# Another order of the pieces on every engine of a fused eight-layer kernel, and spare products at other places

## The chip, the cores and the metric

The kernel runs on one core of a Trainium2 chip. Its time is the device time of one execution in microseconds (us). Each engine works through its own queue strictly in order: TensorE (PE, with its weight loads as PEld), VectorE (DVE), ScalarE (ACT), GpSimd (POOL) and SyncE (SP), which only issues transfers. They wait for one another through semaphores.

## The reference

One sequence of 2048 rows of 128 numbers goes through eight residual layers. Each layer normalises its input and adds its result to it:

```
x = x + attn_a0(layernorm(x))   # delta rule: state S of 8x8 per head, 16 heads, one step per row
x = x + ffn0(layernorm(x))      # shared + 8 experts, top 2
x = x + attn_b0(layernorm(x))   # top 15 of the causal logits, small MLP on them, palette lookup
x = x + ffn0(layernorm(x))
x = x + attn_a1(layernorm(x))   # linear attention, cumulative sums
x = x + ffn1(layernorm(x))      # 8 experts, top 2, relu squared
x = x + attn_b1(layernorm(x))   # decayed state, one step per row
x = x + ffn1(layernorm(x))
```

The first layer is the one that cannot be cut into independent parts:

```
v_old = einsum('bhd,bhde->bhe', k_t, state)
delta = clip(v_t - v_old, -1, 1)
state = state + clip(0.9 * k_t[..., None] * delta[..., None, :], -1, 1)
o     = clip(einsum('bhij,bhj->bhi', state, q_t), -1, 1)
```

## The kernel before

The rows are 16 tiles of 128. All layers are in flight at once, each some tiles behind the one ahead of it. Every stage is a generator for each engine, cut into pieces by `yield`, and a letter stands for each stage: z prep, f front (q, k, v of the first layer), g gram, s scan, o out, a the first expert layer (called ffn0 in the code), p pal (the logits and the top 15), h near (the gathers), m mix, b the second expert layer, l lin, c and e the third and fourth expert layers (ffn1 in the code), d dec. `fast` (line 501) walks through a string of letters, `ORDER[engine]`, and lets the stage of each letter issue its next piece. So five strings set where each piece stands in each queue; within a stage and an engine the pieces keep their order. The engines meet only at semaphores, which are the same whatever the strings say.

The scan (lines 1005 to 1066 on DVE) does the first layer two rows at a time, 1024 steps: L1033 multiplies, L1041 is a tensor_tensor_scan. Four steps are a block. For each block there is a round trip to PE: L1013 (DVE) transposes the last results, L610 (PE) multiplies them with the keys, L1049 (DVE) masks the product, L621 (PE) multiplies that with the keys two blocks on, and L1056 (DVE) adds the result to the values of that later block. L1049 stands after the second step of a block, L1056 after the fourth, so PE has a few steps' time for each. On PE the pieces s with L610 and L621 stand between the pieces of all other stages.

Other lines that are spoken of: L764 (Gram matrices of the gathered rows), L797 and L810 (last products of mix), L831 and L834 (cumulative sums of lin), L564 (transposes of normalised tiles), L871 and L880/L881 (products of the ffn1 experts), L929 and L892 (last products of dec and ffn1), all on PE; L1873 (the gathers, 15 for each tile), L1885 and L1891 (mix), L1733 and L1738 (normalisation), L1898, L1905 and L1914 (lin), L1933 and L1939 (dec) on POOL; L1196 (second search of the top 15), L1220 (clip of mix) and L1249 (adds mix to the tile) on DVE. On SP, L2030 loads the cosines of a tile, L2036 stores its rows of the gather table, L2042 stores its distances, L2053 loads them again for mix, and L2061 stores a finished tile.

`FILL` holds one digit for each of the 2250 pieces on PE. Before each piece `fill(n)` (line 550) sets `idle[0]` to its digit; the next call of `bank` (line 533), which takes one of four PSUM banks in turn, first issues that many spare products (line 541, ones times ones, 128x512, bf16, the result is never read) into the bank and then sets `idle[0]` to 0. The spare products stand after the wait for the bank and ahead of most waits for operands. A piece that takes no bank issues none, and the next piece overwrites its digit.

Of the kernel before, what the change touches and what calls it, by code (L numbers as in the profile page):

```python
# [92 lines left out]
def pieces(stage):  # L93

    for k, _ in enumerate(stage):
# [20 lines left out]
        "smgpmmaplmslmaapmsgmcccmcssccmsmcscsmcmfssmeseeeammsmeseedassedsaesddfdgaaamsddsmmmdpmdbsmbommsbsmpmsmmpsooo"
        "obmbbsmbsbfsbmmslspolossppgslmlllmsallamasmmmsmlmslgmmmsmfcccasmmmscasmaccsccssacafsaeseeespmeemsmdesbedempd"
        "msdssmmbbdpmgsopdmsmmmdddbbobsobsbbooslgfslsmsssllollsloslmsmmpmslglspamspasmcascmsmmccgpmmccsmmcsmcscmasaem"
        "eemsadmemseedfesddadasaesfemdsmdsmmmbmmpmsddgbbsmsmommpsfpbsoosbobsobbsbmmsgsmmsspmlsolmsmosppsmslllmlallsma"
        "fmmgagslmmsmlmfmmcspmsamcccccssaascasaasccgmsmmmseeesemmdmseemmmsmesmdsbdsdbdsebeofspdpdddoobsopbobsgbbbmmss"  # L120
        "lmsmlmsmmsmmsmmmslpslollospppllagamsamspmmlmlfsmgmmcsfcsacascccscsccasasaaseeeesmemedsesedmsesmmdsmdbbmsmdsp"
        "bpggddosmddmmmbosobsbobomsbsbmmsmssmmsplmlosmmmsmposllspmsalslllapsaflssplmmmccmcccgmsmmcmgcscscaaaseeedesmm"
        "meemmmsasaeamsedseddsbdbpbsmpdsdsmmmddmbosbfgboosomosbsbbsfsmmmlslpsmmommsmosppsmllllsallsmsgaaspmfsllmsmggm"
        "mcscccsmmmcpcmascascascaasaeseeseesemmsmdeesdsedsdmmmspmmbdbbpsmdfomdmmddsbbbososbboobfmsgslslsmsmomoslslsml"
        "plsllspmspmlflpsgmcacsmmcmmspcccmmcgsccmsamsaesemesmmmeegdesesedsadsedgsdasammmmmmmdfmdsdadsaasmmsmosmbbbsoo"
        "oospbsbbfpbsmsbbsmmosmsmlsmlsmmmspommsfgmslslslllplmsgmlsmlmspacsmacccscmmsmscascsscspcpgsgemmeemmemmemdmddd"
        "mmseemmmeadsaaseaasgaodsdsddbssbmbssoosoombspbpbsmbbsmmmsmbmpsmmmopolpslsmssmslallalllsmmalmslsmmmcsppcccccs"
        "ccceeeedsmmmmseemmmeaemdsaseadddsaasmammmddbsddsbbommmpmoobpbobobbbmmmmmlpmmmlmspmplllllolopplmalmaammcccccm"
        "mccccaaeedadeddemedemmmmaaeeadsemmmddbdbbpmmmmmpmbmbmbpbbbpmmmpbplmbblmmmmpmmllllbllbmbmbbblmmlmmllcccccclll"
        "llcclcleleedededdemdmemmemmemmmmmcmmmcdmdddcbmbbcmmmmmcmmcmbbcbmbbbcmcmlmdlmmmmededdedelllllleemmmmmmmmedded"  # L130
        "ldelmmmmcccccbbbccccbbebeeedbebbededlldedllllllelldddcdccccccccedeededdedeeeddeddeeeeeeeee",
    "DVE":
# [62 lines left out]
        "lopooloollllllachhmhmhhedhmhhhdhddhdbphhhhpppppbllllllllhhhlhchhlllhlmlmlledhhmhhhdhdchddhbldelmlmllddmdllld"  # L195
# [4 lines left out]
FILL = (  # L200
    "091909062040000000025030020020010000010010000100100000010000500001020020000070000901000001020000000000000020"
# [1974 lines left out]
```

How the kernel before makes its waits and increments, by code:

```python
    def wait_ge(self, sem, val):  # L69
        if self.seen.get(id(sem), 0) < val:
            self.seen[id(sem)] = val
            self.engine.wait_ge(sem, val)
# [460 lines left out]
        def bank(key, *until):  # L533
            b, old = bk.take(key, *until)
            held.extend(old)
            if idle[0]:
                free()
                w.wait_ge(*PV.at("b1", 0))
            for _ in range(idle[0]):
                e.matmul(b[:, 0:512], onesb[:, :], onesb[:, :].unsqueeze(1).to_broadcast([128, 4, 128]), start=True, stop=True)
            idle[0] = 0
            return b
# [1 line left out]
        def free():  # L545
            for sem, val in held:
                w.wait_ge(sem, val)
            held.clear()
# [4 lines left out]
        def norm(s, c):  # L553
            yield
            b = bank((s.name, "T", c), s.A.at("xt", c))
            if s.raw:
                w.wait_ge(*s.src(c))
            elif s.scaled:
                w.wait_ge(*s.A.at("xn", c))
            else:
                w.wait_ge(*s.G.at("xn", c))
            w.wait_ge(*loaded("ident"))
            free()
            e.transpose(b[:, 0:128], X[:, s.tile(c), :] if s.raw else s.xn[c % 2][:, :], ident).then_inc(*s.P("T"))
# [1 line left out]
        def front(c):  # L566
            yield from norm(f, c)
            yield
            b = bank(("front", "qkv", c), f.A.at("pv", c))
            w.wait_ge(*loaded("bias"))
            w.wait_ge(*loaded("cst"))
            free()
            e.matmul(b[:, 0:384], ones, bias[:, 0:384], start=True, stop=False)
```

## Time and profile before

| | us |
|---|---|
| median of 3 runs | 1384.04 (1383.59 to 1386.72) |
| profiled execution | 1393.87 |
| its span in the trace | 1392.1 |
| PE busy | 1243.0 |
| DVE busy | 1000.2 |
| POOL busy | 910.7 |
| ACT busy | 820.1 |

The span is the time from the first instruction to the last; the rest of the profiled execution, 1.8 us, lies around it. A PE record's end is modelled, so a busy PE is not one that works at its peak. The last scan step of the kernel starts 1140.4 us into the span; up to there all stages share the engines, and behind it the last tiles run out.

### The profile page before, as it was taken

The numbers are of one execution on the slowest core, as the hardware profiler recorded it, in microseconds if no ns is written. First come the engines' busy times: TensorE is split into PE (matmuls) and PEld (weight loads), VectorE is DVE, ScalarE is ACT, GpSimd is POOL, SyncE is SP. The second block draws the span as 40 slices with busy tenths as digits, with TensorE's granted clock in tenths as the row PEclk, the third lists the DMA queues.
The fourth block names the chain that finished last, engine by engine and source line by source line (L and its number), as shares of the span: only waits on it lengthen the run. The fifth ranks groups of instructions, "written<-read, shape, count | busy, mean of one in ns | idle before, by whom it ended". The sixth has DMA issues, their size and how long they took to land. (4 is left out here: it accounts for less than half of the span.)

```text
span 1392.1 us, 47171 instructions
## 1 busy us (share of the span) xinstructions
PE 1243.0 (89%) x18561; PEld 813.5 (58%) x18561; DVE 1000.2 (72%) x4437; ACT 820.1 (59%) x2193; POOL 910.7 (65%) x1321
## 2 busy tenths in 40 slices
PE   7777797989999998998899999999999999998896
PEld 3333454656566575756656665755666565757654
DVE  3768878778777868787786888978888775464432
ACT  2232253556676576757476666657574657667764
POOL 5353668686968677685776676776857466674541
PEclk8687678989999999999999999999999999999998
DMA  6000101001000000000010000100001010101000
GB/s 175 2 1 5 30 12 31 24 15 28 12 20 19 16 21 11 24 15 19 14 27 12 15 24 8 29 8 23 15 6 32 6 39 10 34 15 31 4 3 7
DMA packets 27257, 29.35 MB, mean 21 GB/s; under 512 B 12146, under 2 KB 22291, under 8 KB 27027
## 3 DMA queue, kind: packets, MB, share of 16 engines
q0 software_dynamic: 8336, 16.73, 4.9%
q1 hardware_dynamic: 18690, 9.51, 2.5%
q8 instruction: 149, 2.44, 0.8%
q14 instruction: 82, 0.66, 0.2%
HBM read 24.90 MB, written 2.29 MB: 20 GB/s over the span
## 5 line engine op out<-in xcount | busy, mean ns | idle before, releaser
L1873 POOL DMA_INDIRECT sb<-table,sb x240 | 241.8, 1007 | 81.5 <-issue 51.1
L1041 DVE TENSOR_TENSOR_SCAN ps<-ps,sb 128x47 f32<-128x47 f32 (+3 forms) x1024 | 271.0, 265 | 30.5 <-ACT sb L1445 1.5
L1033 DVE TENSOR_TENSOR ps<-sb,ps 128x24 f32<-128x24 f32 (+3 forms) x1024 | 193.1, 189 | 14.7
L541 PE MATMUL ps<-sb 128*128 128x512 bf16 x585 | 177.6, 413 | 8.7 <-ACT sb L1658 2.7
L1733 POOL TENSOR_TENSOR sb<-sb 128x1 f32<-128x1 f32 x128 | 73.2, 574 | 138.3 <-DVE sb L976 137.6
L610 PEld LDWEIGHTS ps<-sb 32*32 32x32 f32 x2032 | 41.0, 108 | 107.6 <-DVE sb L1013 65.6
L610 PE MATMUL ps<-sb 32*32 32x32 f32 x2032 | 69.8, 209 | 36.2 <-DVE sb L1013 35.6
L621 PEld LDWEIGHTS ps<-sb 32*32 32x32 f32 x2032 | 41.5, 108 | 93.1 <-DVE sb L1049 54.3
L982 DVE TENSOR_TENSOR sb<-ps,sb 128x128 f32<-128x128 f32 x112 | 32.2, 289 | 80.5 <-PE ps L708 29.8
L541 PEld LDWEIGHTS ps<-sb 128*128 128x128 bf16 x585 | 54.7, 105 | 58.8 <-issue 14.5
L1369 ACT ACTIVATE sb<-ps 128x128 f32<-128x128 f32 x128 | 34.9, 275 | 90.7 <-PE ps L564 90.2
L621 PE MATMUL ps<-sb 32*32 32x12 f32 x2032 | 64.7, 189 | 19.0 <-DVE sb L1049 10.0
L1056 DVE TENSOR_TENSOR ps<-sb,ps 128x12 f32<-128x12 f32 x254 | 40.9, 161 | 51.7 <-PE ps L621 50.3
L708 PE MATMUL ps<-sb 128*128 128x128 f32 x512 | 77.3, 298 | 0.0
L1670 ACT ACTIVATE sb<-ps,sb 128x128 bf16<-128x128 f32 x256 | 70.8, 375 | 8.2 <-PE ps L881 8.0
L596 PE MATMUL ps<-sb 128*128 128x480 f32 x128 | 73.8, 665 | 1.4 <-DVE ps L1056 0.5
L1049 DVE TENSOR_TENSOR sb<-ps,sb 128x32 f32<-128x32 f32 x254 | 45.9, 181 | 39.2 <-PE ps L610 38.1
L1885 POOL TENSOR_TENSOR sb<-sb 128x512 f32<-128x512 f32 (+1 forms) x32 | 47.3, 1485 | 36.0 <-DVE sb L1239 35.8
L764 PE MATMUL ps<-sb 128*16 128x16 f32 x4096 | 64.6, 211 | 6.3 <-issue 4.2
L708 PEld LDWEIGHTS ps<-sb 128*128 128x128 f32 x512 | 68.9, 209 | 1.9 <-issue 1.1
L1772 POOL TENSOR_TENSOR sb<-sb 128x480 f32<-128x480 f32 x64 | 66.0, 1034 | 4.9 <-ACT sb L1408 4.3
L764 PEld LDWEIGHTS ps<-sb 128*16 128x16 f32 x4096 | 54.3, 133 | 24.8 <-issue 18.4
(313 smaller groups left out, 3532.3 us busy)
## 6 DMA issues: line engine op xcount, KB each, us to landing
sb<-table,sb POOLq DMA_INDIRECT x240
sb<-in_cs SPq DMA_DIRECT2D x16, 128.0 KB
table<-sb SPq DMA_DIRECT2D x17, 64.0 KB, 1.5
sb<-dscr SPq DMA_DIRECT2D x64, 2.0 KB
out<-sb SPq DMA_DIRECT2D x16, 64.0 KB, 1.6
sb<-in_x SPq DMA_DIRECT2D x3, 256.0 KB, 5.4
sb<-in_wex SPq DMA_DIRECT2D x1, 512.0 KB, 4.1
sb<-in_rvx SPq DMA_DIRECT2D x1, 512.0 KB, 4.5
```

Of the source, the lines that this page charges most:

```text
L541: e.matmul(b[:, 0:512], onesb[:, :], onesb[:, :].unsqueeze(1).to_broadcast([128, 4, 128]), start=True, stop=True)
L596: e.matmul(b[:, 0:32 * LW], blk, g_.pp[j % 2][:, :], start=True, stop=True).then_inc(*g_.P("s"))
L610: x = e.matmul(psS[rows, 0:32], KZT[c % 2][rows, 32 * o1:32 * o1 + 32], R[g % 2][rows, :], start=g == 0, stop=True, skip_group_check=True)
L621: x = e.matmul(b[rows, 0:12], SB[g % 2][rows, :], KM[c2 % 2][rows, 4 * o2:4 * o2 + 4, :].rearrange("p a b -> p (a b)"), start=True, stop=True)
L708: x = e.matmul(b[:, 0:128], s.hw[j // 4][:, 128 * (j % 4):128 * (j % 4) + 128], wex[:, 128 * j:128 * j + 128], start=False, stop=j == 7)
L764: x = e.matmul(pb[32 * q:32 * q + 16, 16 * k:16 * k + 16], PTt[:, at, :], PTt[:, at, :], start=True, stop=True)
L1033: e.tensor_tensor(at(psP, p + ROW - 3 - 2 * m, [ROW, 3], [2, m], [1, 2]), AC[:, row(n, k), :, HIST - 2 * m:HIST].rearrange("p r (a b) -> p ...
L1041: e.tensor_tensor_scan(at(psD, 16 + k + COMB * skip, [COMB, 3 * ROW - skip]), at(psP, p + skip, [1, 3 * ROW - skip]), Q[:, i % 32, skip:3 ...
L1670: x = e.activation(s.w[:, 128 * at:128 * at + 128], bk.of[s.name, "d", g, c][:, 128 * j:128 * j + 128], ACT.Copy, scale=t[:, 40 + at:41 + at])
L1733: e.tensor_tensor(st[:, 11:12], st[:, 10:11], mhalf[:, 0:1], ALU.pow).then_inc(*s.G("lr"))
L1772: e.tensor_tensor(g_.pp[j % 2][:, :].rearrange("p (a b c) -> p a b c", b=2, c=LW), at(KT[c % 3], 32 * j, [2, 16], [0, 2], [1, LW]), km[:, ...
L1873: e.indirect_dma_start(GA[:, k, :], None, table[0:128 * i + 128, :] if i else table0, bass.IndirectOffsetOnAxis(u[:, k:k + 1], 0)).then_in ...
```

## The change

Both tables are replaced, `ORDER` and `FILL`; no other line changes. Each string of `ORDER` holds the same letters in the same numbers (2250 on PE, 3861 on DVE, 1707 on ACT, 996 on POOL, 80 on SP). 897 pieces of PE, 1419 of DVE, 866 of ACT, 585 of POOL and 55 of SP stand at another place, most of them one or two places on.

```diff
 ORDER = {
...
     "POOL":
...
-        "cbedllllldllldddceddddde",
+        "cbedllllllllddddceddddde",
     "SP":
-        "ppppmpppmpppmppmpppmppppmppppmppmppppmpmpppppmpmpppmppepemeppppmpeepemeeeeeeeeee",
+        "pppppmpmpppppmpmppppmpppmeppmppeppmpppmpppmpppepmepmpeppmppepmpppeppmepmeeeeeeee",
 }
 FILL = (
...
```

The digits of `FILL` add up to 585 before and to 1242 now. All 585 stand at pieces that take a bank. Of the 1242, 587 do; the other 655 stand at pieces that take none, and are overwritten.

On PE, some 850 us into the span, in the part where all stages run. L610 and L621 are the scan's two products, L764 and L831/L834 belong to mix and lin. Before:

```order
L736 MATMUL ps<-sb 128x512 x2
L610 MATMUL ps<-sb 32x32 x4
L764 MATMUL ps<-sb 16x16 x16
L831 MATMUL ps<-sb 128x432
L834 MATMUL ps<-sb 128x432
L831 MATMUL ps<-sb 128x360
L834 MATMUL ps<-sb 128x360
L621 MATMUL ps<-sb 32x12 x4
```

And now:

```order
L736 MATMUL ps<-sb 128x512 x2
L610 MATMUL ps<-sb 32x32 x4
L831 MATMUL ps<-sb 128x432
L834 MATMUL ps<-sb 128x432
L621 MATMUL ps<-sb 32x12 x4
L764 MATMUL ps<-sb 16x16 x16
L564 MATMUL ps<-sb 128x128
L831 MATMUL ps<-sb 128x360
```

The 16 products of L764 and one pair of L831 and L834 (360 columns) moved from ahead of the scan's L621 to behind it.

On PE, some 655 us into the span; L871 and L564 belong to the last ffn1 and to dec, L797 and L810 to mix. Before:

```order
L871 MATMUL ps<-sb 128x128 x4
L797 MATMUL ps<-sb 32x16 x16
L564 MATMUL ps<-sb 128x128
L797 MATMUL ps<-sb 32x16 x8
L610 MATMUL ps<-sb 32x32 x4
L871 MATMUL ps<-sb 128x128 x8
L797 MATMUL ps<-sb 32x16 x8
L541 MATMUL ps<-sb 128x512 x3
L810 MATMUL ps<-sb 32x128 x16
L621 MATMUL ps<-sb 32x12 x4
```

And now:

```order
L797 MATMUL ps<-sb 32x16 x8
L871 MATMUL ps<-sb 128x128 x4
L810 MATMUL ps<-sb 32x128 x8
L871 MATMUL ps<-sb 128x128 x4
L610 MATMUL ps<-sb 32x32 x4
L810 MATMUL ps<-sb 32x128 x8
L621 MATMUL ps<-sb 32x12 x4
```

The scan's L610 moved behind the last eight of L797, behind both groups of L871 and behind the first eight of L810, and three spare products are gone from this place.

On POOL, 1263 to 1272 us into the span, the last gathers of the last tile (L1873). Before:

```order
L1933 COPY sb<-sb 128x4
L1873 DMA sb<-table,sb 128x128
L1939 TENSOR_TENSOR sb<-sb 128x4x128
L1733 TENSOR_TENSOR sb<-sb 128x1
L1738 TENSOR_SCALAR sb<-sb 128x128
L1873 DMA sb<-table,sb 128x128
L1933 COPY sb<-sb 128x4
L1939 TENSOR_TENSOR sb<-sb 128x4x128
L1873 DMA sb<-table,sb 128x128
```

And now:

```order
L1933 COPY sb<-sb 128x4
L1939 TENSOR_TENSOR sb<-sb 128x4x128
L1873 DMA sb<-table,sb 128x128 x2
L1733 TENSOR_TENSOR sb<-sb 128x1
L1738 TENSOR_SCALAR sb<-sb 128x128
L1933 COPY sb<-sb 128x4
L1873 DMA sb<-table,sb 128x128
L1939 TENSOR_TENSOR sb<-sb 128x4x128
```

The last gather stands ahead of the second L1939 instead of behind it.

## Rows read from the trace of the kernel before

**Rows 1.** The page: busy time of PE and DVE, and the spare products' group.
```profile
PE 1243.0 (89%) x18561; PEld 813.5 (58%) x18561; DVE 1000.2 (72%) x4437; ACT 820.1 (59%) x2193; POOL 910.7 (65%) x1321
...
L541 PE MATMUL ps<-sb 128*128 128x512 bf16 x585 | 177.6, 413 | 8.7 <-ACT sb L1658 2.7
```

**Rows 2.** Four stretches: PE, PEld, DVE, ACT, POOL busy, clock, DMA share, GB/s.
```profile
0.00:315.00 315.00, 253.85 (x3249) 141.28 (x3253) 230.53 (x1194) 121.80 (x341) 191.95 (x326) 0.79 0.13 33
315.00:1141.00 826.00, 766.83 (x12286) 517.86 (x12287) 655.65 (x2926) 533.20 (x1416) 588.68 (x837) 0.97 0.07 19
1141.00:1314.00 173.00, 159.61 (x2564) 113.02 (x2563) 88.90 (x236) 119.20 (x306) 109.44 (x133) 1.00 0.08 20
1314.00:1392.00 78.00, 62.71 (x471) 41.34 (x471) 25.12 (x84) 45.87 (x132) 20.67 (x27) 0.95 0.02 5
```

**Rows 3.** Scan steps (L1041) in two early stretches: busy time (count), clock.
```profile
35.00:70.00 35.00, 12.75 (x48) 0.67 0.01 2
70.00:105.00 35.00, 9.60 (x36) 0.84 0.01 1
```

**Rows 4.** Timeline of PE late in the span: five spare products in a row.
```profile
1357.73 1.24 PE L541 MATMUL ps<-sb 128*128 128x512 bf16 x5
```

**Rows 5.** Waits of DVE for the scan's products, whole span: us, times, longest.
```profile
DVE ps L1056 <- PE ps L621: 50.3, 65, 3.1
...
DVE sb L1049 <- PE ps L610: 38.1, 52, 4.8
```

**Rows 6.** Timelines at 850 us: PE, then DVE; in brackets idle before, releaser.
```profile
850.58 0.77 PE L831 MATMUL ps<-sb 128*128 128x360 f32 x2
...
851.88 0.25 PE L621 MATMUL ps<-sb 32*32 32x12 f32 x8
...
852.20 0.18 DVE L1056 TENSOR_TENSOR ps<-sb,ps 128x12 f32<-128x12 f32 x1 [1.90 <-PE ps L621]
```

**Rows 7.** Timelines at 655 us: PE, then DVE.
```profile
655.44 0.26 PE L610 MATMUL ps<-sb 32*32 32x32 f32 x8
...
657.34 1.10 PE L810 MATMUL ps<-sb 32*32 32x128 f32 x32
...
656.17 0.17 DVE L1049 TENSOR_TENSOR sb<-ps,sb 128x32 f32<-128x32 f32 x1
...
659.05 0.18 DVE L1056 TENSOR_TENSOR ps<-sb,ps 128x12 f32<-128x12 f32 x1 [1.70 <-PE ps L621]
```

**Rows 8.** The chain that ended last, at the last gather: start, us, what.
```profile
1269.45 1.18 POOL sb L1939
...
1270.78 2.64 DMA sb<-table,sb
1273.46 0.66 PE ps L751 x4
```

**Rows 9.** The same chain where mix of the last tile ends.
```profile
1309.00 0.71 PE ps L929 x4
...
1311.43 1.95 PE ps L810 x64
```

**Rows 10.** Timeline of POOL at 1340 us.
```profile
1339.42 1.13 POOL L1933 COPY sb<-sb 128x4 f32<-128x4 f32 x1
...
1344.56 0.18 POOL L1933 COPY sb<-sb 128x4 f32<-128x4 f32 x1
```

**Rows 11.** SP's issues at 143 and 184 us, and the clip that waits.
```profile
143.15 2.46 SPq L2053 DMA_DIRECT2D sb<-dscr  x4
184.69 0.34 SPq L2036 DMA_DIRECT2D table<-sb  x1
...
190.22 0.74 DVE L1220 SCALAR_TENSOR_TENSOR sb<-ps,sb 128x512 f32<-128x512 f32 x1
```

**Rows 12.** The last tile: its second search (timeline of DVE), a later gather (chain).
```profile
1239.29 2.29 DVE L1196 FIND_INDEX8 sb<-sb 128x8 uint32<-128x2048 f32 x1
...
1255.88 0.94 POOL sb L1873
```

More of the change, by code:

```diff
@@ L116 @@
[L116 to L120, printed above, removed]
@@ new lines @@
+    "ACT":
+        "ffffffffffgfgfsffsffzzgfffgzffgfzsfzsfgzfffggszfffsfzfgooozooffoozffgoffaazasaaagassgpppfppffffpsopgopofoopo"
+        "posgoaaaaasaafpffmfgmpsfpmmopgfpppffffpoooosoommfmsgomamfmppafpfaaapaffmmasgpmgpsooooosofffffommmmppoppgpsaa"
+        "apfagaapmmsgpmmamfpmfbffbbmmbbbbpsfpmlollgooooloslfffffomlmmmgplpppoppccfcccccppacccccsagccamadmfaaspmmdddda"
+        "dfmffgmmfmbsbgbbobbffffgofpbompoosoolllgmomfmlpplmpalgppplaaasgacpccccsacccmccccmpccmmfeepeeeeaeedeemeedemed"
+        "dmddmfffsgbbfobmbbppbooobomosoffmmfffmfplpolplppplagallalasaampgpmmcpmfccaccccscmcmcccccmmffefeseeeeeeedbeed"
+        "eebeddddfbbbpmgpbobooosooolgfflffflmllolmmppmsaplgpapapfcccaacccccgamcccmpccmcsmaeedeeeeedemsemddeefededmmeb"
+        "ffffbpmgbbpobbpffspffbfoooooommgmmplppposlflppalallafgaagamlmmmpfcfafccsccmcmcccccccpmmcfpgeedeeeemeeesedbee"
+        "eddbddbebbfofbffpfsbooopogoommlmmllpppolplpfppsalamagaammmlafgcmcfcffmsccacccccccpccmmeeeedeeeeebeseedeeddfb"
+        "ddbppbbpbggmoboooooosmmmmspplppllolpaapllpafffaaalffmcmmcpcmcccccgccccmcgcmmameeedeeeesdeeeeeeesddpdbfdbpbbb"
+        "mpbbofgoooooomfffmlsmmpsplpolpppafllalagaapfalffffmmmspggmccccccccccamcmcccmmeeedeeeeeeepeebsdeeddddpmbfbbbs"
+        "pofbboooooofffmlgllmmompplflpslpapplfpffffgcccccccaccmccsmccpcgammeadeeeaaeeefdeegeemeeepddsmaddmgmmfobbbbbb"
+        "oooopboofffpsfmmmmsollpplpfpfgfffllplmagmlmfmcpacaccccccsccmmaccaccmppmageegeeeeeddeeddseedmeedmapeobgbbmbbb"
+        "soooomobppompppoplpplalsmmallalmmalaamcpsccpcccccccccmccmmeeedeedeeeeeeeeaeddddmpbbbbbommbpmmobopoopopolpllm"
+        "mpppllolppalmaamcacaccccacmccccmcccmamedeedddeeddeeeeeeeeembbpbbpbpbmbmmpmpppbppblpbbblblpmmlbllmmllmmllcccc"
+        "ccccclcclccclmmleedeedeeeddeededeeeemcpcmmcmcbbcmbbbccbcccbccmccmlmmddllmmdeededdeememleleeeleemeelcccbccccb"
+        "ccbcbbcbcccbeeedeeeeeedeeddelellddellllccccccccccccccdeedeeeeddeddeeeeeeeeeeeeeeeeeeeee",
@@ L219 @@
[L219 to L221 removed]
+    "903199061040000000025030024120103000010010000000100103010020500001120020030070000900000130020000103200000020"
+    "200002000200000003000000000000401000000002100500002100034000000002300610000030004320010000000030040020000000"
@@ new lines @@
+    "101003000020000010000311013011301200013030003301100000000020030103102000000000100401200520000000000000000210"
+    "000000000000320003023300011400000000030000000000001300000003000600000110000300201000000000000002030033030000"
+    "000400000030000000202200100000000000004010072600020000030100000000000000000000000000030000000000000000000000"
+    "000000000000000000003000000220100120000000001000374050000600020000200000004000000100101000009000000000600060"
+    "300000000000000020000020000000000700000040001100000000200000000000000000003022000000003010303003120330020000"
@@ new lines @@
+    "000000000007000000000014000000005000030000020002200023000101004002000000000010000000000000000100100000000100"
+    "000001000003000000000000000000000000000000000000006210001633000000000000000000000000000000000000000002000000"
+    "000000200000000000000010000000500000002101000101012000000010000007502000100000000000013800030000000000000000"
+    "400000000007130000000003000000000000200004000200000000000100001000000020000510000040006030030000103002200020"
+    "000000001000000000000000000000020000000000000000400000003000000000000702020002010000060026303030800106000020"
```

173 lines of the change are left out of this document (75 added, 98 removed).

## The prediction

> **What bounds the kernel now.** I read the page's busy times first: PE is busy for 1243.0 of 1392.1 us and DVE for 1000.2 [rows 1]. A busy share over the whole span hides where the time goes, so next I cut the span at the end of the scan and at two points beside it [rows 2]. From 315 to 1141 us, where all stages run, PE is busy for 766.8 of 826 us (93%) and DVE for 655.7 (79%). In this part PE comes nearest to a bound, and the scan on DVE is the chain that it must not hold up. Up to 315 us PE is busy for 253.9 (81%) and DVE for 230.5 (73%). Behind 1141 us there is no scan; the chain of waits runs back through POOL, PE and single transfers there [rows 8, 9], and from 1314 us every engine but PE is less than 60% busy: that is one tile's latency.
>
> The view of waits then tells what DVE waits for: in the whole span 50.3 us for L621 (65 times) and 38.1 us for L610 (52 times), the two products of the scan's round trip [rows 5]. These 88.4 us are the largest sum that an order on PE can give back to the scan, and any product put ahead of L610 or L621 can add to it.
>
> **The spare products.** The change speaks of 1242 in place of 585. A digit of the table counts only where its piece takes a bank; counted in the two built orders, L541 stands 585 times before and 587 times now. Five of them in a row take 1.24 us [rows 4], 0.25 us each, so the two more cost 0.5 us of PE at most, and where PE waits anyway they cost nothing; I take 0. If all 1242 were issued, 655 x 0.25 = 164 us of products would go into a PE that idles for 149 us in all; that case is shut out by the order. Most digits that did change place moved with a neighbour, because two pieces changed places and the product stands with the first bank taken.
>
> The clock belongs here, since the products keep PE at work. The granted clock is 0.79 up to 315 us and 0.97 from there to 1141 us [rows 2]. With the levels 1.2 and 2.4 GHz that is 2 x 0.21 x 315 = 132 us and 2 x 0.03 x 826 = 50 us at the lower one. What does it cost? From 35 to 70 us the clock is 0.67 and 48 scan steps are done; from 70 to 105 us it is 0.84 and only 36 are done [rows 3]. So early on the clock does not set the pace, and I price it at 0 there. In the middle, with PE at 93%, the 50 us can cost up to half of themselves, 25 us. The Trainium skill, "TensorE: Matmul & The Clock Gate", section "HAM oscillation — how this bites in real kernels", puts the cost of throttled time at half of it wherever it falls. By that rule the early 132 us would cost 66 us and each early spare product would be worth having; rows 3 speak against it for this kernel.
>
> **The moves on PE.** For each scan product that DVE waited for I set the work that the new order takes from ahead of it, or puts there, at its duration in the trace, with what that work waits for held at its old time. Three results come of it, of which one sample each can be followed.
> - Products that come earlier. At 850 us, L621 loses 16 of L764 and a pair L831/L834 from ahead of it. The pair alone takes from 850.58 to 851.88, 1.3 us; with L764 it is 1.7 us of the 1.90 us for which DVE waited [rows 6]. Capped at its wait each time, this sums to 13.6 us over the span.
> - Waits that grow: 5.7 us, none above 1.4 us.
> - New waits where there was none: 11.3 us over 21 places. The largest in this sum, 3.3 us, is at 655 us: L610 went behind two groups of L871 and eight of L810. L810 could not start before 657.34, and L1049 took the product at 656.17 [rows 7]. Read on, though: the eight of L810 (half of 1.10 us) and four of L871 end at about 658.2, so L1049 comes at 658.5, 2.3 us late; the 1.70 us for which L1056 waited after it vanish in this, and L1056 comes at 659.7 in place of 659.05. Of 3.3 us, 0.65 are left.
>
> So a gain stays, while a loss is partly swallowed by the next wait. I take the gains in full and the losses (17.0 us) at a third, between the fifth of the sample and all: 13.6 - 5.7 = 7.9 us. Of these I let half reach the end, since the scan shares its pace with PE, which saves no work: -4.0 us. The ends are -13.6 (all gains, no loss) and +17.0 (the reverse).
>
> **The moves on POOL behind the scan.** The last gather of the last tile is issued at 1270.78, right behind L1939 (1.18 us); it lands 2.64 us later and PE takes it at 1273.46 [rows 8]. The new order puts L1939 behind the gather: 1.2 us earlier. Late next is the previous tile: L929 waits for POOL's products of dec until 1309.00, and L810 of the last tile, 1311.43, stands behind L929 [rows 9]. The new order leaves this sequence on PE. So between 0 and 1.2 us come through; I take 0.6. At 1339.42 a copy of four columns, L1933, takes 1.13 us, six times the 0.18 us of its like at 1344.56 [rows 10]. Three L1914 stood behind it; it now stands behind them. That is worth 0 to 1.1 us; I take 0.5 us, since L1939 of the dec layer comes later by as much and ends against the same normalisation. Sum -1.1 us.
>
> **Moves priced at nothing, with their cover.** SP stores finished tiles from 480 us on instead of from 1082 us; each add that it waits for is done before the next transfer of SP is due, so nothing queues behind it. The first L2053 moves from 143.15 behind the L2036 of 184.69: four issues of 2.46 us end at 187.5, and L1220 reads at 190.22 [rows 11]. That leaves 2.7 us for the landing; if it takes longer, L1220 and the scan step behind it wait, up to 2 us. On DVE, the first part of an expert pick, which ran behind the second search (L1196, 1239.29 to 1241.58) before, now stands ahead of it. I allow it until the time at which it ran, so the search ends some 4.5 us later, at 1246; the first gather that needs it is issued at 1255.88 [rows 12], and POOL is busy with other pieces until then. All other moves on ACT, POOL and DVE take 0; bounded by the nearest rows, the PE sums above, -13.6 to +17.0 us.
>
> **Sum.** 1393.87 - 4.0 - 1.1 = 1388.8 us in terms of the profiled execution. That one ran 0.7% above the median of the runs, 1384.04; in their terms the sum is 1388.8 x 1384.04 / 1393.87 = 1379.0 us.
>
> **The rivals.**
> 1. Nothing that can be measured: gains and losses on the scan cancel. For it: the sums are 13.6 and 17.0 us, and the work is the same on each engine. Against it: the swallowed loss at 655 us. Time 1384.
> 2. Slower: the scan's products stand behind work that waits for another engine. The place is PE from 640 to 1090 us; besides 655 us, an L610 near 784 us now follows L845, L773, L779 and L564, which wait for ACT and for an add. With all losses counted (17.0) and all gains (13.6) it is +3.4 us, with half the gains (6.8) it is +10.2; the middle, +6.8, gives 1400.7, in the runs' terms 1391. It decides once a late product isn't followed by a wait that was there already, as the one at 659.05 was [rows 7]. Against it: 16 of the 21 new waits are under 0.6 us.
> 3. The clock. If the spare products at their new places hold the clock for 20 of the 50 us at 1.2 GHz between 315 and 1141 us, half of that comes back: 1383.9, or 1374. The same can go the other way (from 1066 to 1150 us there are 12 fewer of them): +7 us, 1391.
>
> **How the numbers follow.** No change means within 0.2% (2.8 us), about what a measurement of this kernel can tell. The forecast has 0.34, its own range is 1372 to 1381; the clock as a gain has 0.10: faster 0.44. Rival 1 has 0.27. Rival 2 has 0.22 and the clock as a loss 0.07: slower 0.29. The range goes from 1368 (gains of 13.6 in full and a little of the clock) to 1394 (rival 2 with half the gains): about one in ten is left out on each side.
>
> **What would show it.** The waits of DVE for L621 and L610 should sum to 80 us or less in place of 88.4; the wait of 1.90 us at 850 us should be gone, and near 655 us L1049 should wait for L610 by about 2 us with no wait at L1056 behind it. The last scan step should start some 4 us ahead of 1140.4. L541 should stand 587 times. Of the last two L1939 ahead of the last gather one should be left behind it. I am wrong if these waits sum to 90 us or more (rival 2), if the clock from 315 to 1141 us leaves 0.97 by more than 0.01 (rival 3), or if the last scan step comes early and the end doesn't: then the tail after 1141 us gave it back.

## The result and the profile after

The changed kernel takes 1397.81 us (median of 17 runs, 1392.61 to 1407.67), the kernel before 1389.32 us beside it (17 runs, 1383.17 to 1398.24). The ratio is 1.0069, with a 95% interval of 1.0051 to 1.0088: slower by 0.7%, where I had forecast 1379 us and faster (a ratio of 0.996 to the 1384.04 us of before that I started from). The time lies 4 us beyond the end of the range. Of the 18.8 us between forecast and measurement 5.3 are not the change's: the kernel before itself took 1389.32 us in these 17 runs and 1384.04 in the three ahead of the prediction.

The two profiled executions are no measure of this difference. That of before took 1393.87 us, 4.5 us above its median, and that of the changed kernel 1393.32 us, 4.5 us below its own. So I read from the traces where time moved, and from the timed runs how much.

First the page of the changed kernel, which answers to [rows 1]:

```profile
PE 1235.9 (89%) x18563; PEld 818.3 (59%) x18563; DVE 998.7 (72%) x4437; ACT 821.2 (59%) x2193; POOL 904.9 (65%) x1321
```

L541 stands 587 times in the changed kernel's list of groups, as counted. DVE is busy for 998.7 us in all, a little less than the 1000.2 of before: whatever slows the kernel isn't a larger sum of work on DVE. Next the four stretches, which answer to [rows 2]:

```profile
0.00:315.00 315.00, 253.13 (x3380) 142.39 (x3384) 235.38 (x1221) 125.34 (x355) 194.95 (x336) 0.82 0.13 33
315.00:1141.00 826.00, 761.58 (x12162) 519.54 (x12152) 648.09 (x2887) 531.19 (x1400) 577.90 (x824) 0.96 0.07 18
1141.00:1314.00 173.00, 159.46 (x2572) 114.65 (x2571) 90.09 (x249) 119.00 (x308) 111.27 (x136) 1.00 0.07 19
1314.00:1392.00 78.00, 61.76 (x469) 41.76 (x468) 25.19 (x83) 45.69 (x132) 20.75 (x27) 0.95 0.02 5
```

Up to 315 us DVE has done more than before (1221 instructions for 1194), from 315 to 1141 us less (2887 for 2926). At 1.2 GHz (twice the missing share of the granted clock, times the length) the trace of before has 198 us in all, this one 195. From 315 to 1141 us alone it is 57 us before and 72 now (0.97 and 0.96), 15 more. Some 12 of these lie behind scan step 609, where this trace is no slower (the table below), and 3 in the stretch where the time is lost. So the loss is in the middle, and it is hardly the clock. The view of DVE's waits answers to [rows 5]:

```profile
DVE ps L1056 <- PE ps L621: 46.1, 59, 3.5
DVE sb L1049 <- PE ps L610: 41.3, 60, 3.3
```

They sum to 87.4 us, where before had 88.4 and I had named 80 or less. Both sampled places moved the way that I had worked out, but less far. Of the wait of 1.90 us near 850 us [rows 6], which should have gone, 0.67 is left, and near 655 us [rows 7] L1049 now waits, 1.07 us in place of about 2, and L1056 no longer does (groups of one instruction: start, duration, in brackets the idle time before it and its releaser):

```profile
854.02 0.17 DVE L1056 TENSOR_TENSOR ps<-sb,ps 128x12 f32<-128x12 f32 x1 [0.67 <-PE ps L621]
```

```profile
661.33 0.19 DVE L1049 TENSOR_TENSOR sb<-ps,sb 128x32 f32<-128x32 f32 x1 [1.07 <-PE ps L610]
...
662.93 0.17 DVE L1056 TENSOR_TENSOR ps<-sb,ps 128x12 f32<-128x12 f32 x1
```

**Where the scan falls behind.** The scan has 1024 steps (L1041), in one order in both kernels, so the start of step n can be set against the start of step n. Worked out from these starts, for the kernel before, the changed one and some of the experiments below (us for each part):

```
steps        before  changed  changed, again (e5)  e9     e10    e11    e12
0 to 357     306.6   300.6    305.5                304.7  302.0  301.0  301.1
357 to 383   28.3    30.0     28.4                 30.0   28.3   29.8   29.5
383 to 391   10.6    13.2     13.6                 13.2   10.6   13.2   11.0
391 to 577   220.5   223.9    223.8                226.6  222.8  222.9  220.3
577 to 586   10.9    13.3     14.9                 13.8   10.9   13.7   10.9
586 to 609   21.5    22.5     22.5                 21.9   22.3   21.7   22.9
609 to 1023  517.0   514.3    514.4                512.2  513.8  514.8  510.6
```

e9 has the new order from about step 357 to 609 alone and e10 the old order there alone; e11 has the new order around the two short places of steps 383 to 391 and 577 to 586 alone, e12 the old order around these alone. So in the first row e9 and e11 are in the old order, as before is: the same order took between 301.0 and 306.6 us, and the 6 us that the changed kernel is ahead at step 357 in its trace can't be put down to the change. With the 2.7 us of the last row and 3.0 behind the scan they hide its loss in this one trace, whose whole span is no longer than that of before (1391.5 for 1392.1 us).

Steps 357 to 609 (331.6 to 623.4 us in the trace of before) take 291.8 us before and 302.8 after. Here are this window and two short ones, of the two places, of before, then of the changed kernel, with the busy time of the scan steps alone in them (252, 8 and 9 steps) and the clock:

```profile
331.60:623.40 291.80, 66.45 (x252) 0.97 0.07 18
359.90:370.50 10.60, 2.12 (x8) 1.00 0.03 8
591.00:601.90 10.90, 2.38 (x9) 1.00 0.08 20
```

```profile
325.70:628.50 302.80, 66.56 (x252) 0.97 0.07 18
355.70:368.90 13.20, 2.08 (x8) 0.92 0.06 16
592.70:606.10 13.40, 2.38 (x9) 1.00 0.11 28
```

The same steps, the same busy time, 11 us more around them at the same clock. Two short places make 5.0 of it. There DVE is busy for longer and idle for less: 12.4 and 0.7 us for 8.9 and 1.7 at the first, 12.4 and 0.9 for 9.7 and 1.2 at the second. Outside them it is idle for longer; over the whole of steps 357 to 609 the waits for L621 and L610 sum to 21.8 us for 18.7. What DVE does at the second, first in the changed kernel and then in the kernel before:

```profile
593.32 0.27 DVE L1041 TENSOR_TENSOR_SCAN ps<-ps,sb 128x51 f32<-128x51 f32 x1
593.50 0.15 DVE L1144 MAX8 sb<-sb 128x8 f32<-128x8 f32 x1
593.56 1.78 DVE L1147 SCALAR_TENSOR_TENSOR sb<-sb 128x256 f32<-128x256 f32 x1
595.27 0.28 DVE L1249 TENSOR_TENSOR sb<-ps,sb 128x128 f32<-128x128 f32 x1
595.47 3.03 DVE L1152 SCALAR_TENSOR_TENSOR sb<-sb 128x256 f32<-128x256 f32 x1
598.42 0.19 DVE L1033 TENSOR_TENSOR ps<-sb,ps 128x42 f32<-128x42 f32 x1
```

```profile
592.13 0.42 DVE L1147 SCALAR_TENSOR_TENSOR sb<-sb 128x256 f32<-128x256 f32 x1 [0.61 <-ACT sb L1493]
...
592.84 0.88 DVE L1152 SCALAR_TENSOR_TENSOR sb<-sb 128x256 f32<-128x256 f32 x1
```

DVE is "busy" here and no wait is shown, but one instruction of one shape takes 0.42 us in one trace and 1.78 in the other, and the next 0.88 and 3.03. (The trace of before isn't free of this at the place: L1130 takes 1.11 us in it, at 595.17, and 0.17 in the changed kernel.) POOL in the changed kernel at this time:

```profile
593.45 1.03 POOL L1772 TENSOR_TENSOR sb<-sb 128x480 f32<-128x480 f32 x1
594.43 0.63 POOL L1760 TENSOR_TENSOR sb<-sb 128x256 f32<-128x256 f32 x1
595.02 0.76 POOL L1780 TENSOR_TENSOR sb<-sb 128x224 f32<-128x224 f32 x1
595.75 0.42 POOL L1784 TENSOR_TENSOR sb<-sb 128x16 f32<-128x16 f32 x2
596.13 2.08 POOL L1795 TENSOR_TENSOR sb<-sb 128x512 f32<-128x512 f32 x2
598.37 0.98 POOL L1873 DMA_INDIRECT sb<-table,sb  x1 [0.16 <-issue]
```

Seven instructions without a gap, from 593.45 to 598.21 us. L1152 starts at 595.47 and ends at 598.50, 0.29 us behind the last. Here is POOL in the kernel before. L1152 started at 592.84 there, beside L1780, and ended at 593.72, ahead of both L1795; L1760 took 0.86 us for the 0.63 above:

```profile
592.39 0.59 POOL L1780 TENSOR_TENSOR sb<-sb 128x224 f32<-128x224 f32 x1
592.95 0.42 POOL L1784 TENSOR_TENSOR sb<-sb 128x16 f32<-128x16 f32 x2
593.34 0.86 POOL L1760 TENSOR_TENSOR sb<-sb 128x256 f32<-128x256 f32 x1
594.16 2.09 POOL L1795 TENSOR_TENSOR sb<-sb 128x512 f32<-128x512 f32 x2
```

The Trainium skill, "SBUF — State Buffer", section "Who interferes with whom", has the rule: a DVE instruction with two inputs in SBUF contends with a GpSimd (POOL) instruction that reads SBUF, and one of the two is blocked whole. The traces agree as to which instructions: at the two places L1147, L1152, L1130 and L1132 are the stretched ones, all sb<-sb, while L1249 and the scan's own, with an operand in PSUM (ps), keep their times. The first place is alike. In the changed kernel POOL runs there from 359.53 to 365.18 us without a gap; L1152 takes 1.33 us at 359.57 (0.38 before), and L1130 and L1132, 128x8 each, take:

```profile
362.03 1.28 DVE L1130 TENSOR_TENSOR sb<-sb 128x8 f32<-128x8 f32 x1
363.35 1.86 DVE L1132 TENSOR_TENSOR sb<-sb 128x8 f32<-128x8 f32 x1
```

where the trace of before has 0.17 us for each. The scan's steps stand behind them in DVE's queue. The four stretched lines together take 3.7 us more than before at the first place and 2.6 us more at the second, and the places last 2.6 and 2.4 us longer.

### The profile page after: what moved, and what is told of

It reads as the page before. It is cut to its first block, busy times and chain, and to the rows that moved or that the text cites. A ratio compares the mean times of both kernels' runs of the same rounds, so it can differ in the third digit from the quotient of the medians.

```text
span 1391.5 us, 47171 instructions
## 1 busy us (share of the span) xinstructions
PE 1235.9 (89%) x18563; PEld 818.3 (59%) x18563; DVE 998.7 (72%) x4437; ACT 821.2 (59%) x2193; POOL 904.9 (65%) x1321
## 4 chain that ended last, share of the span: by engine, by line
PE 47%; POOL 19%; DVE 13%; issue 11%; ACT 8%; SPq 1%; DMA 1%; POOLq 0%; DVEq 0%; ACTq 0%
POOL sb L1873 5%; PE ps L541 4%; PE ps L708 3%; PE ps L764 3%; DVE ps L1041 3%; PE ps L596 2%; DVE ps L1033 2%; PE ps L621 2%; POOL sb L1733 2%; PE ps L831 2%; PE ps L610 2%; PE ps L736 2%; PE ps L640 2%; PE ps L788 2%; POOL sb L1885 1%
## 5 line engine op out<-in xcount | busy, mean ns | idle before, releaser
L1041 DVE TENSOR_TENSOR_SCAN ps<-ps,sb 128x47 f32<-128x47 f32 (+3 forms) x1024 | 271.7, 265 | 30.1 <-ACT sb L1445 1.1
L1873 POOL DMA_INDIRECT sb<-table,sb x240 | 242.6, 1011 | 75.8 <-issue 52.3
L541 PE MATMUL ps<-sb 128*128 128x512 bf16 x587 | 177.0, 412 | 6.9 <-ACT sb L1572 1.4
L610 PE MATMUL ps<-sb 32*32 32x32 f32 x2032 | 69.5, 208 | 38.0 <-DVE sb L1013 36.2
L610 PEld LDWEIGHTS ps<-sb 32*32 32x32 f32 x2032 | 40.5, 107 | 104.3 <-DVE sb L1013 61.8
L621 PEld LDWEIGHTS ps<-sb 32*32 32x32 f32 x2032 | 41.5, 108 | 97.9 <-DVE sb L1049 56.0
L621 PE MATMUL ps<-sb 32*32 32x12 f32 x2032 | 64.9, 188 | 26.4 <-DVE sb L1049 15.1
L541 PEld LDWEIGHTS ps<-sb 128*128 128x128 bf16 x587 | 54.0, 104 | 56.1 <-issue 14.9
L1049 DVE TENSOR_TENSOR sb<-ps,sb 128x32 f32<-128x32 f32 x254 | 46.0, 181 | 42.7 <-PE ps L610 41.3
L1056 DVE TENSOR_TENSOR ps<-sb,ps 128x12 f32<-128x12 f32 x254 | 40.8, 161 | 47.3 <-PE ps L621 46.1
L764 PE MATMUL ps<-sb 128*16 128x16 f32 x4096 | 63.5, 211 | 5.2 <-issue 3.9
L764 PEld LDWEIGHTS ps<-sb 128*16 128x16 f32 x4096 | 53.8, 133 | 23.7 <-issue 17.2
```

The costliest lines, as they stand in the source:

```text
L541: e.matmul(b[:, 0:512], onesb[:, :], onesb[:, :].unsqueeze(1).to_broadcast([128, 4, 128]), start=True, stop=True)
L610: x = e.matmul(psS[rows, 0:32], KZT[c % 2][rows, 32 * o1:32 * o1 + 32], R[g % 2][rows, :], start=g == 0, stop=True, skip_group_check=True)
L621: x = e.matmul(b[rows, 0:12], SB[g % 2][rows, :], KM[c2 % 2][rows, 4 * o2:4 * o2 + 4, :].rearrange("p a b -> p (a b)"), start=True, stop=True)
L764: x = e.matmul(pb[32 * q:32 * q + 16, 16 * k:16 * k + 16], PTt[:, at, :], PTt[:, at, :], start=True, stop=True)
L1041: e.tensor_tensor_scan(at(psD, 16 + k + COMB * skip, [COMB, 3 * ROW - skip]), at(psP, p + skip, [1, 3 * ROW - skip]), Q[:, i % 32, skip:3 ...
L1873: e.indirect_dma_start(GA[:, k, :], None, table[0:128 * i + 128, :] if i else table0, bass.IndirectOffsetOnAxis(u[:, k:k + 1], 0)).then_in ...
```

## The experiments

Three theories at first: M, the scan's products on PE wait in the middle, C, the spare products and the clock, and T, the tail behind the scan. Then, for the spare products apart from the order: O, the order makes the loss by itself, B, the new places of the spare products are worse, and J, spare products cost when moved away from the order that they stand in. Last W and P (the loss sits between 331 and 623 us, in the two places above) against J. Hybrids were cut by the trace: a piece is in the new order if it ran in the window, and its digit goes with it. "Chip A" below stands for the chips on which the kernel before takes 1390 us, as where the change was timed, "chip B" for those on which it takes 1454 to 1460 us. Each ratio is to the kernel before in the same group, on the same chip, with its 95% interval.

**e1 to e4, parts of the change on the kernel before (chip B).** The edit of e1 starts so in PE's string; e2 and e3 are alike further on, and e4 changes only the table of digits:

```diff
 "PE":
-"sfffsggffssgzzgssfssgsfsssszsgsssfzsssszssgssszssgsfsszsgoszoosossssfzfgssozossosasasasgsssaassasasasasgsssp"
+"fssffggffssgzzgssfssgsfsssszsgsssfzsssszssgssszssgssfszsgoszoosossssfzfgsoszossosasasasgsssaasassasasasgsssp"
...
 FILL = (
-"091909062040000000025030020020010000010010000100100000010000500001020020000070000901000001020000000000000020"
+"903199061040000000025030024120103000010010000000100103010020500001120020030070000900000130020000103200000020"
...
```

> The kernel before, with the new order of PE, DVE, ACT and POOL and its spare products only for the pieces that ran up to 315 us; every later piece, and SP, stands as before. The loss of the whole change is 0.69%, some 9 us. Theory M (the loss comes from the scan's products between 315 and 1066 us, where the changed kernel fell 8 to 10 us behind in the two traces): this one is 0 to 4 us faster, ratio 0.997 to 1.000, since the changed kernel was 4 us ahead at 315 us. Theory C (the clock: other places of the spare products cost something wherever they move): slower by its share, some 2 us, ratio 1.001 to 1.003. Theory T (the tail): 1.000.

> The kernel before, with the new order and the spare products that go with it only for the pieces that ran from 315 to 1066 us. Theory M (the scan's products wait there): nearly the whole loss is in here, 7 to 11 us, ratio 1.005 to 1.008. Theory C (clock): two thirds of it, ratio 1.003 to 1.005. Theory T (tail): 1.000.

> The kernel before, with the new order and its spare products only for the pieces that ran from 1066 us on. The prediction took 1.1 us off for the two moves on POOL here. Theory M: ratio 0.998 to 1.000. Theory T (the tail carries the loss; it has 18 spare products less than before): ratio 1.004 or more. Theory C: 1.001 to 1.003.

> The order of before on every engine; only the table of spare products is the new one, each digit on the piece on which the changed kernel has it (587 are issued, some 1 in 3 of them at another piece). Theory M and the prediction: no effect, 0.999 to 1.001. Theory C (the spare products and the clock): it carries the loss, ratio 1.004 or more; if it carries part of it, the ratio is that part.

Measured: e1 1476.07 us, ratio 1.0096 (1.0063 to 1.0128); e2 1507.20, 1.0319 (1.0294 to 1.0344); e3 1473.30, 1.0084 (1.0061 to 1.0107); e4 1474.22, 1.0084 (1.0055 to 1.0112). No theory had all of this (C named e4's, T e3's): each part costs, and the middle more than three times as much as the whole change on chip A. The baseline, 1460.48 us, says that something else is at work. It is seen in PE's waits; here those of e4, whose order is that of before (waiter, releaser: us in total, times, longest):

```profile
PE ps L797 <- issue: 9.3, 17, 1.2
PE ps L610 <- issue: 4.8, 6, 1.2
PE ps L788 <- issue: 4.8, 9, 1.2
PE ps L764 <- issue: 4.7, 6, 1.5
```

"Issue" is idle time in which the engine waited for nothing that the profile shows. The trace of before on chip A has 4.2 us of it at L764, 1.6 at L788 and none at L797. So these four say little of the loss on chip A.

**e5 to e8, the order and the spare products apart (chip A).** e5 is the changed kernel once more; e6 has its order with the digits of before on their pieces; e7 and e8 have none:

```diff
 FILL = (
-"091909062040000000025030020020010000010010000100100000010000500001020020000070000901000001020000000000000020"
+"000000000000000000000000000000000000000000000000000000000000000000000000000000000000000000000000000000000000"
...
```

> The changed kernel itself, unaltered, beside the other kernels of this group, since the kernel before took 1460 us on the chip of the first group and 1389 us on the one where the change was timed. All theories: ratio about 1.007 if the loss is the same on this chip; on the chip of the first group, where parts of the change cost 0.8 to 3.2%, it may be up to 1.02.

> The order of the changed kernel on every engine, with the spare products of before, each on the piece on which it stood before (585 issued). Theory B (the new places of the spare products are simply worse): this one is back at 1.000 to 1.003. Theory J (the spare products are fitted to the order that they stand in, and cost when moved away from it): it is slower than the changed kernel, 1.010 or more. Theory O (the order makes the loss and the spare products don't matter): it is the same as the changed kernel.

> The kernel before with none of its 585 spare products. Left out is work whose results nothing reads. By the prediction the products cost nothing and the clock is worth up to 25 us in the middle: 1.00 to 1.03. If time at 1.2 GHz costs a third of itself, as the scatter over the runs of the first group says (0.12 to 0.48 us of span for each us at the lower clock), and such time grows from 200 to some 500 us: ratio 1.05 to 1.10.

> The changed kernel with none of its 587 spare products. With e7 it compares the two orders alone. Theory O (the order): it is 0.5 to 1% slower than e7. Theories B and J (the spare products and the clock): the two are equal within 0.3%, or this one is faster, as the waits that the prediction summed would have it (-4 us, -0.3%).

Measured: e5 1402.87 us, 1.0094 (1.0057 to 1.0131); e6 1407.04, 1.0115 (1.0075 to 1.0155); e7 1450.32, 1.0427 (1.0393 to 1.0460); e8 1450.23, 1.0427 (1.0396 to 1.0459). e6 takes theory B away: the old digits don't help the new order. Its ratio is what J asked for (1.010 or more) and, within the noise, also that of the changed kernel, as O had it. e7 and e8 are equal, each to about 0.35%. That is what J had said, and not O, which had e8 slower by 0.5 to 1%: without spare products a loss of the order of up to some 0.5% could hide there, but hardly all of 0.94%. In single traces e8 is still 0.8 and 2.5 us slower than e7 at the two places above (15.9 for 15.1, 15.9 for 13.4), with L1152 at 3.03 us for 0.87 at the second; why the whole kernels are equal all the same is open. e7 came out between its two stated ranges (up to 1.03, and from 1.05). They also price the clock. e7 in the four stretches:

```profile
0.00:315.00 315.00, 227.18 (x3168) 135.30 (x3168) 232.14 (x1199) 123.10 (x346) 193.57 (x328) 0.74 0.13 33
315.00:1141.00 826.00, 732.80 (x11519) 514.98 (x11509) 618.86 (x2810) 512.88 (x1351) 560.38 (x805) 0.88 0.07 17
```

Over its runs e7 has 483 us at 1.2 GHz, before 195 beside it (twice the missing share of the granted clock times the span, mean of the runs). The span grows by 60 us for these 288: 0.21 us for each, with the gain from 585 products less already taken off. Early, DVE does as much in 315 us at 0.74 (1199) as before did at 0.79 (1194), so the price of 0 there stands; from 315 to 1141 us it does 116 instructions fewer.

**e9 to e12, windows of the order (chip A).** e9 is the kernel before with the new order at 331 to 623 us, e10 the changed kernel with the old order there; e11 and e12 are the same pair for the two places alone. At the second place e11 moves on POOL:

```diff
-L1772 TENSOR_TENSOR sb<-sb 128x480
-L1873 DMA sb<-table,sb 128x128
-L1780 TENSOR_TENSOR sb<-sb 128x16x14
-L1784 TENSOR_TENSOR sb<-sb 128x16 x2
-L1760 TENSOR_TENSOR sb<-sb 128x256
+L1873 DMA sb<-table,sb 128x128
+L1772 TENSOR_TENSOR sb<-sb 128x480
+L1760 TENSOR_TENSOR sb<-sb 128x256
+L1780 TENSOR_TENSOR sb<-sb 128x16x14
+L1784 TENSOR_TENSOR sb<-sb 128x16 x2
 L1795 TENSOR_TENSOR sb<-sb 128x512 x2
```

The gather (L1873), which had stood inside the row of tensor instructions, now stands ahead of it, and seven of them follow one another. On DVE L1144 goes behind three more scan steps and L1147 behind one more, and both come to stand beside this row.

> The kernel before, with the new order of PE, DVE, ACT and POOL and its spare products only for the pieces that ran from 331 to 623 us (scan steps 357 to 609), which took 291.8 us before and 302.8 to 304.8 us in three traces of the new order. Theory W (the loss is made in this part and stays): 8 to 12 us slower than before, ratio 1.006 to 1.009. Theory J (the loss is that of any order that the spare products were not fitted to, wherever it is): the ratio says nothing of this part, and this kernel and e10 are both slower than before, by 1.005 or more.

> The mirror of e9: the changed kernel, with the order and the spare products of before only for the pieces that ran from 325 to 628 us. Theory W: it loses nothing, ratio 0.997 to 1.002. Theory J: as slow as the changed kernel or slower, 1.007 or more.

> The kernel before, with the new order only for the pieces that ran at 355 to 371 us and at 586 to 606 us, where two-input instructions of DVE on SBUF wait behind unbroken chains of POOL in the new order (L1152 takes 3.03 us at 595 us and 0.88 before; L1130 and L1132 take 1.28 and 1.86 us at 362 us and 0.17 each before). Theory P (these places): the stretched L1152 is seen again, the two places together cost 5 to 8 us, ratio 1.003 to 1.006. Theory J: stretched instructions may be there, but the time is anywhere. No effect of them on the end: 1.000 to 1.002.

> The mirror of e11: the changed kernel with the order of before only for the pieces at 350 to 369 us and at 586 to 608 us. Theory P: it wins back 5 to 8 us of the changed kernel's loss, ratio 1.001 to 1.004, and L1152 near 595 us is under 1 us. Otherwise it stays at 1.007 to 1.009.

Measured: e9 1399.91 us, 1.0074 (1.0059 to 1.0089); e10 1393.20, 1.0026 (1.0009 to 1.0044); e11 1392.23, 1.0025 (1.0010 to 1.0040); e12 1391.80, 1.0013 (0.9993 to 1.0033). Theory W has e9 where it expected it and e10 just outside; J, which wanted both at 1.005 or more, has only e9. The changed kernel (1.0069, 1.0094) with 763 of some 8800 places in the four strings put back is within 0.2 to 0.3% of before. And e12, with 76 places put back, wins back at least as much as e10 with ten times as many, within the noise of the two. (The changed kernel wasn't timed beside them; its 1.0069 and 1.0094 come from two other groups with the same time of before, 1389 to 1390 us.) e11 brings in 3.5 us of what e12 takes away: the lower end of its range missed by a little, so in the old order the places cost about half. On this chip the longest L1152 follows the order at the place. All L1152 from 320 to 640 us (shortest, median, longest in ns), in e11 and in e12:

```profile
L1152 DVE SCALAR_TENSOR_TENSOR sb<-sb x9: 414/424/3032, 329.7 to 629.0; 128x256 f32<-128x256 f32 x9
```

```profile
L1152 DVE SCALAR_TENSOR_TENSOR sb<-sb x9: 381/424/877, 330.0 to 622.9; 128x256 f32<-128x256 f32 x9
```

The median is one and the same; only the longest moves, 3.03 us with the new order at the place and 0.88 with the old. The waits of e12 on DVE, beside [rows 5]:

```profile
DVE ps L1056 <- PE ps L621: 40.5, 57, 3.0
DVE sb L1049 <- PE ps L610: 38.3, 55, 3.3
```

They sum to 78.8 us, below the 80 that I had named (e10: 81.8; changed and e5: 87.4 and 88.2). So in the new order part of these waits goes with the two places. That doesn't hold the other way: e11, which has the places in the old order, sums to 85.6, less than the 88.4 of before. Nor is it shown that the places cost time behind them as well: steps 391 to 577 take 223.9 us in the changed kernel and 220.3 in e12, but 222.8 in e10, with the old order there and at the first place.

DVE's busy time on the page says the same of the places in both orders. It is 1003.4 us in e11 for 1000.2 before, and 994.5 in e12 for 998.7 and 1000.2 in the two traces of the changed order. It also shows what the ratios leave unexplained:

```profile
PE 1232.0 (89%) x18557; PEld 815.4 (59%) x18557; DVE 994.5 (72%) x4437; ACT 820.8 (59%) x2193; POOL 902.3 (65%) x1321
```

e12 has 5.7 us less on DVE than before, and 9.6 us less in the waits for the scan's products, and still is no faster (1.0013). Something else in the new order gives this back. It wasn't found.

**e13 to e18, which engines at the two places, and a better kernel (chip B).** e13 and e17 are one kernel, e12 with only DVE and POOL put back; e14 puts back only PE and ACT; e15 is e12 with the old order from 1143 us on; e16 and e18 are e15 with the old order also from 369 to 451 and 861 to 891 us. Of e13 the edit on DVE at the first place:

```diff
-"sssssssssdsssddsssdsmsfsmaassssssssssssssmssssabssdssssssssfsssssssssssssbsssssssssssbpbsbbssfbsssbfssssbsss"
+"sssssssssdsssddsssdsmsfsmaassssssssssssssmsssabssssdsssssssfsssssssssssssssssssssssbsbpbbbsfsssfbsbsssssbsss"
```

> e12 with less in it: the changed kernel with the order of before only on DVE and POOL, only for the pieces at 350 to 369 us and 586 to 608 us; PE, its spare products and ACT stay new. Theory P (the loss at the two places is DVE's two-input SBUF instructions standing behind POOL's chains): the whole gain of e12 is here, ratio 1.000 to 1.003, and the sum of L1130, L1132 and L1152 from scan step 357 to 609 is back to 10 us from 13. Theory Q (it is PE's order at these places): ratio stays at 1.006 to 1.009.

> The other half of e12: order of before only on PE (with its spare products there) and ACT at the two places; DVE and POOL stay new. Theory P: ratio 1.005 to 1.009, L1152 near 595 us takes 3.03 us again. Theory Q: 1.000 to 1.003.

> e12 and also the order and the spare products of before for all pieces from 1143 us on, behind the scan. In single traces the stretch from the last scan step to the end took 251.6, 251.5 and 250.0 us with the old order there and 248.6, 252.4, 252.0 and 253.1 with the new. If the prediction's -1.1 us for this stretch is right, this one is 1 us slower than e12 (ratio 1.002); if the traces are, it is 1 us faster (1.000), which is less than five rounds can tell, so the trace decides.

> A version meant to beat both: e15, with the order of before also from 369 to 451 us and from 861 to 891 us, where the new order lost 2.0 and 2.1 us in the trace of e12 against before. If such local losses and gains add up: scan steps end 12 us ahead of before (e12: 8.8), ratio 0.993 to 0.998. If an order is only good as a whole with its spare products: 1.002 or more.

> The kernel of e13 once more: its group ran on a chip on which the kernel before took 1454 us and every kernel in the new order 3.6 to 4.5% more, so it could not be set against e12, which ran where before takes 1390 us. On such a chip, theory P (DVE behind POOL's chains): ratio 1.000 to 1.003. Theory Q (PE's order at the two places): 1.006 to 1.009. From the traces of e13 and e14, where each half took back a part (scan steps 383 to 391 took 11.56 and 12.02 us; 13.2 with all new, 10.6 with all old), a third: half of the gain, 1.003 to 1.006.

> The kernel of e16 once more, for the same reason. If local losses and gains add up: the last scan step is 10 to 14 us ahead of that of before, ratio 0.993 to 0.998. If an order is only good as a whole with its spare products: 1.002 or more.

Measured: e13 1521.22 us, 1.0437 (1.0394 to 1.0481), and e17 1518.72, 1.0444 (1.0413 to 1.0474); e14 1522.89, 1.0447 (1.0399 to 1.0494); e15 1510.01, 1.0389 (1.0346 to 1.0433); e16 1505.04, 1.0356 (1.0309 to 1.0403), and e18 1498.89, 1.0313 (1.0279 to 1.0347). Both groups fell on chip B, where all kernels in the new order lose 3 to 4.5%, so no range for a gain was met (e16 and e18 lie in their other range, 1.002 or more, which on chip B says nothing). What is left is their order and their traces. Steps 383 to 391 and 577 to 586 take 12.1 and 13.9 us on chip B with the new order on all engines (e2), 12.0 and 13.4 in e14, 11.6 and 12.5 in e13, and 10.6 and 10.9 in e15 with all four engines put back. Each half takes back a part, DVE and POOL more of it, and neither the whole. L1152 at the second place tells why an order on DVE and POOL alone doesn't settle it. In e13 both are in the old order, and from 320 to 720 us the longest is 2.73 us (2.72 in e17):

```profile
L1152 DVE SCALAR_TENSOR_TENSOR sb<-sb x9: 380/424/2730, 364.2 to 687.6; 128x256 f32<-128x256 f32 x9
```

It starts at 652.85 us there, beside L1760 on POOL (652.62), and ends at 655.58, behind both L1795; in the trace of before it had started beside L1780 and ended ahead of them. By these traces what decides is when the two engines meet, and not their own two orders alone. That DVE and POOL alone would win the change back on chip A was not measured. No kernel here beat the kernel before.

## Why the prediction was wrong

- **The step that failed** is in the moves priced at nothing: "All other moves on ACT, POOL and DVE take 0". I bounded them by sums on PE and asked of each moved instruction only what waits for it. I didn't ask what else runs while it runs. Putting the old order back at two places, 76 of the changed places, gives 0.6 to 0.8% back (e12 at 1.0013 against 1.0069 and 1.0094), about the whole loss; the new order at these places alone costs 0.25% (e11). At once they cost 2.6 and 2.4 us. On DVE, steps 357 to 609 hold 5.5 us more of busy time (236.3 for 230.8) and 5.5 us more of idle time. The trace of before already showed such a stretch (L1152 0.88 us at 592.84, with another of its kind at 0.38). The Trainium skill, "SBUF — State Buffer", section "Who interferes with whom", has the rule. That the order at these places costs the time is shown. That it does so by the stretched instructions is read from the traces, where they account for the 5.0 us at once; that these 5.0 become the 8 to 11 us of e12 is not explained. The places hold moves on all four engines, and putting back two of the four took back only a part (e13, e14). Nor is it the sum of the stretches over the kernel: DVE is busy for 1.5 us less than before in all.
- **Spare products: right in count, right that going back to the old digits doesn't help on chip A** (e6), though "cost 0" can't be shown to a few us, and by e7 and e8 the loss may need the spare products to show. On chip B the table alone costs 0.84% (e4); why is open.
- **Clock: right that it would not decide.** 195 us at 1.2 GHz in the changed kernel's trace, 198 in that of before; at the 0.21 us of e7 the 15 us more in the middle would be 3 us. The price in the middle was bounded by a half; over the whole span e7 says a fifth, with the gain from the missing products taken off.
- **Moves on PE (-4.0 us): the samples right in their direction, the gain isn't there.** e12, with nearly all of these moves and without the two places, is at 1.0013 (0.9993 to 1.0033), where the forecast was 0.996. So the places account for the loss, and this term for the rest of the miss. Its step was that half of what DVE waits less reaches the end: in e12 DVE waits 9.6 us less for the two products, and nothing reaches it. From step 609 to 1023 the new order takes 514.3, 514.4, 513.8 and 510.6 us (changed, e5, e10, e12) and the old one 517.0, 512.2 and 514.8 (before, e9, e11): no clear difference. The last scan step came 2.5 and 6.6 us behind 1140.4 in the traces of the changed kernel and of e5; in e12 it came 8.8 us ahead, in an execution of 1386.5 us, which is quicker than e12's median.
- **Tail (-1.1 us): the moves are there, the gain isn't seen.** One L1939 stands behind the last gather, and L1933 takes 0.19 us in place of the 1.13 of [rows 10]:

```profile
1268.34 1.09 POOL L1873 DMA_INDIRECT sb<-table,sb  x1 [0.18 <-issue]
1269.46 1.19 POOL L1939 TENSOR_TENSOR sb<-sb 128x512 f32<-128x512 f32 x1
```

```profile
1343.18 0.19 POOL L1933 COPY sb<-sb 128x4 f32<-128x4 f32 x1
```

  From the last scan step to the end it is 251.6, 251.5 and 250.0 us with the old order (before, e9, e11) and 248.6, 252.4, 252.0 and 253.1 with the new (changed, e5, e10, e12): no difference that these show.
- **The rivals.** Rival 2 named the right side and nearly the right place (PE from 640 to 1090 us; it was 331 to 623), but its mechanism, products on PE, has at most a part: the waits for these products grow by 3.1 of the 11 us from step 357 to 609, they are no longer than before over the whole span (87.4 for 88.4 us), and at the two places DVE waits less than before. Rival 3 fell with the clock.

## What to carry over

When an order moves, look at what runs beside each moved instruction, not only at what waits for it: a row of POOL's tensor instructions on SBUF without a gap can hold up a DVE instruction with two SBUF inputs to its end (3.03 us for 0.42 here), and all that stands behind it on DVE waits too. In the trace this isn't a wait but a busy instruction that is longer than its like, so compare the shortest, the median and the longest of a line before taking its mean as a price. A smaller sum of such stretches, or of waits, is no gain by itself: e12 has less of both than before and isn't faster. And where two orders differ by under 1%, time them on more than one chip: the order that lost 0.7% on one lost 3% or more on another.

## What the runs showed of the hardware

- **A blocked instruction can be passed over more than once.** L1147 at 593.56 us got through in the middle of POOL's row, as its end at 595.34 shows; L1152 at 595.47 did not until the row ended at 598.21. In one it is 1.4 us of waiting, in the other 2.6. What decides that, no run here shows.
- **It works the other way too.** L1780 takes 0.76 us at 595.02 beside L1147, and 0.56 us at 365.06 in the trace of before.
- **A stretch repeats from run to run on one kind of chip.** Steps 383 to 391 take 13.2, 13.6, 13.2 and 13.2 us with the new order (changed, e5, e9, e11) and 10.6, 10.6 and 11.0 with the old (before, e10, e12), though the executions differ by up to 15 us. With no spare products the same steps take 15.1 us in the old order (e7), 6.2 of them idle, and none of the four lines is stretched there.
- **Chips differ in how long PE stands still without a wait.** On chip B this idle time sums to 32 to 52 us of the span, on chip A to 5 to 9, and much of it is inside rows of small matmuls. In e13, near 1230 us (from 1228 to 1237 us L797 has 8 such idle times):

```profile
1228.21 0.25 PE L797 MATMUL ps<-sb 64*32 64x16 f32 x5 [0.48 <-issue]
1228.95 0.24 PE L797 MATMUL ps<-sb 64*32 64x16 f32 x4 [0.49 <-issue]
1229.66 0.18 PE L797 MATMUL ps<-sb 64*32 64x16 f32 x1 [0.47 <-issue]
```

  and over its whole span:

```profile
PE ps L797 <- issue: 14.2, 27, 1.1
PE ps L788 <- issue: 8.0, 19, 0.6
PE ps L764 <- issue: 7.7, 14, 1.4
PE ps L621 <- issue: 5.7, 9, 1.4
```

  L797 has no such time in the trace of before on chip A. The durations of DVE, ACT and POOL are the same on both (DVE busy for 1000.2 us in before, 1001.0 in e1). That instructions come late there is my reading, not shown; why they hit the new order harder is open.
